# A vision-transformer tower on one core: by-query products and maxima 14 steps ahead of the by-key products in place of 16, and a head's maxima turned in its third step

## The reference

```python
h = _L0_tok_ref(x, ...)                       # gated token mixing, PReLU
h = h + _L0_attn_ref(_layernorm(h, axis=-1), ...)
h = h + _L0_ffn_ref(_layernorm(h, axis=-1), ...)   # 8 experts, top 2

# inside _L0_attn_ref, per image and head
attn = jnp.einsum('bnhd,bmhd->bhnm', q * scale, k)
attn = jax.nn.softmax(attn + bias[None], axis=-1)
out = jnp.einsum('bhnm,bmhd->bnhd', attn, v)
```

## Time and profile before

| | |
|---|---|
| Median of 3 runs | 548.75 us |
| The profiled execution's own time | 552.72 us |
| Its span | 550.9 us |
| Busy share over the span | PE 95%, DVE 83%, ACT 64%, POOL 16% |
| Share of the chain that ended last | PE 81%, DVE 8%, DMA 3%, issue 3% |
| Mean granted TensorE clock | 0.983 of full speed |

### The profile page before, as it was taken

One profiled execution on the slowest core, in us unless ns is written; L12 is line 12 of the kernel. 1 busy time (PEld: TensorE's weight loads), 2 busy tenths in 40 slices (PEclk: granted clock), 3 DMA queues, 4 the chain that ended last, 5 costly groups with the idle time before them and its releaser, 6 DMA issues.

```text
span 550.9 us, 12866 instructions
## 1 busy us (share of the span) xinstructions
PE 525.9 (95%) x4185; PEld 178.9 (32%) x4185; DVE 455.9 (83%) x539; ACT 355.0 (64%) x631; POOL 86.7 (16%) x184
## 2 busy tenths in 40 slices
PE   7999999889999999999999999999999989999996
PEld 5233333322333333333333333333333443233221
DVE  2678778987999999999999999999999676766644
ACT  2021222327898988988988989889888745445442
POOL 8701011324100001001001010010012340211000
PEclk9999999997999999999999999999999978999999
DMA  7600358691332323223223223233244000100001
GB/s 277 186 4 2 87 162 234 162 284 22 90 78 73 80 77 84 78 61 89 79 61 87 75 75 79 69 85 78 60 132 109 22 11 11 43 20 1 20 14 26
DMA packets 51095, 45.28 MB, mean 82 GB/s; under 512 B 26265, under 2 KB 39034, under 8 KB 51066
## 3 DMA queue, kind: packets, MB, share of 16 engines
q1 hardware_dynamic: 51066, 44.89, 29.0%
HBM read 28.70 MB, written 16.17 MB: 81 GB/s over the span
## 4 chain that ended last, share of the span: by engine, by line
PE 81%; DVE 8%; issue 3%; DMA 3%; SPq 2%; ACT 1%; POOL 1%; DVEq 0%; ACTq 0%; POOLq 0%
PE ps L1456 25%; PE ps L1352 13%; PE ps L1441 13%; PE ps L1533 5%; PE ps L1613 5%; PE ps L1275 4%; PE ps L1286 4%; DVE nmax L910 2%; DVE gated L931 1%; SPq L431 1%; PE ps L1445 1%; PE ps L1366 1%; PE ps L1600 1%; DMA maxima<-max_t 1%; DMA q_ring<-maxima 1%
## 5 line engine op out<-in xcount | busy, mean ns | idle before, releaser
L910 DVE TENSOR_REDUCE nmax<-ps 128x1 f32<-128x1024 f32 x256 | 302.2, 1218 | 19.8 <-PE ps L1352 11.3
L763 ACT ACTIVATE probs<-ps 128x512 f32<-128x512 f32 x512 | 278.1, 596 | 56.3 <-PE ps L1441 46.5
L1456 PE MATMUL ps<-probs,v_ring 128*32 128x256 f32 x2048 | 166.3, 398 | 0.0
L1441 PE MATMUL ps<-q_ring,k_ring 51*128 51x512 bf16 x512 | 101.8, 387 | 6.3 <-DMA q_ring<-maxima 2.0
L1352 PE MATMUL ps<-k_ring,q_ring 48*128 48x512 bf16 x512 | 100.5, 389 | 1.0 <-DVE nmax L910 0.7
L1456 PEld LDWEIGHTS ps<-probs,v_ring 128*32 128x32 f32 x2048 | 40.7, 108 | 63.8 <-issue 38.0
L1183 DVE TENSOR_TENSOR probs<-probs,ps 128x1024 f32<-128x1024 f32 x32 | 39.0, 1220 | 25.1 <-PE ps L1600 19.6
L1352 PEld LDWEIGHTS ps<-k_ring,q_ring 48*128 48x128 bf16 x512 | 24.6, 92 | 106.4 <-issue 99.4
L779 ACT ACTIVATE probs<-ps,wide_w 128x1024 f32<-128x1024 f32 x32 | 35.4, 1113 | 33.6 <-PE ps L1533 32.5
L931 DVE SCALAR_TENSOR_TENSOR gated<-ps,v_s,gamma_sb 128x1024 f32<-128x1024 f32 x32 | 40.8, 1281 | 12.3 <-PE ps L1275 10.9
L605 POOL TENSOR_TENSOR max_p<-nmax,zeros 128x8 bf16<-128x8 f32 x32 | 6.4, 200 | 274.7 <-DVE nmax L910 260.9
(11 more groups left out here) (168 smaller groups left out, 338.7 us busy)
## 6 DMA issues: line engine op xcount, KB each, us to landing
k_ring<-qk_parts SPq DMA_DIRECT2D x64, 96.0 KB, 2.4
q_ring<-qk_parts SPq DMA_DIRECT2D x64, 96.0 KB, 2.4
gamma_sb<-gamma_t SPq DMA_DIRECT2D x4, 1024.0 KB, 8.8
v_padded<-v_pad SPq DMA_DIRECT2D x4, 1024.0 KB, 5.8
v_ring<-v_padded SPq DMA_DIRECT2D x32, 128.0 KB, 3.2
outputs<-o_t SPq DMA_DIRECT2D x32, 128.0 KB
qk_parts<-qk_h SPq DMA_DIRECT2D x8, 384.0 KB, 4.6
x_ring<-bias_parts SPq DMA_DIRECT2D x32, 96.0 KB, 3.0
```

Of the source, the lines that this page charges most:

```text
L763: A.activation(probs[:, s % 4, HALF * j:HALF * (j + 1)], ps[:, key_bank(s, j), :], ACT.Exp).then_inc(exp_done[j], 1)
L910: V.tensor_reduce(nmax[:, par, s:s + 1], ps[:, bank:bank + 2, :].rearrange("p a n -> p (a n)"), AX, ALU.max, negate=True).then_inc(s1_redu ...
L1441: last = mm(ps[:, key_bank(s, j), :], k_ring[rows, u, P * s:P * (s + 1)], q_ring[rows, u, HALF * j:HALF * (j + 1)], start=True, stop=not c ...
L1456: last = mm(ps[VC * j:VC * (j + 1), PVB, 0:2 * P], v_ring[:, u, m, :], probs[:, m % 4, 2 * P * j:2 * P * (j + 1)], start=(m == 0), stop=(m ...
```

## The change

By-query products and their reductions run `LEAD = 14` steps ahead of the by-key products. Steps 0 and 1 of head g now carry by-query steps 6 and 7 of head g+1, and steps 2 to 7 carry steps 0 to 5 of head g+2. Two by-query steps fewer stand ahead of the loop, and head 30 carries the last two. The turn of head g+1's maxima moves from step 0 of head g to step 2. The place where the rows are waited for (step 7) stays, and so does SP's program. The first projection of the next stage is issued whole in step 2 of head 30, and no longer in two halves in steps 1 and 2. In after, a line number behind the added lines is 5 or 6 higher.

```diff
--- before.py
+++ after.py
@@ -295,6 +295,11 @@
         out_stored = [sem(f"out_stored{i}") for i in range(2)]
 
         N_OPERANDS = 5
+        LEAD = 2 * NT - 2
+
+        def by_query(s):
+            return 1 + (s + LEAD - NT) // NT, (s + LEAD) % NT
+
         N_MAX_ROWS = 16
         S1A, S2A, PVB = 0, 4, 7
 
@@ -1023,7 +1028,7 @@
             rest_part(B - 1)
             first_maxima(6, 9)
             turn_maxima(0, 0, None)
-            first_maxima(9, 2 * NT)
+            first_maxima(9, LEAD)
 
 
             def invert_sums(b):
@@ -1057,11 +1062,12 @@
                 for u in range(RING):
                     g = it * RING + u
                     for s in range(NT):
-                        if not (last and u >= RING - 2):
-                            if s == 0:
-                                dve.wait_ge(max_split, g + 1)
-                            row_max(g + 2, s, u % 2)
-                        if s == 0 and not (last and u == RING - 1):
+                        ahead, step = by_query(s)
+                        if not (last and u + ahead >= RING):
+                            if step == 0:
+                                dve.wait_ge(max_split, g + ahead - 1)
+                            row_max(g + ahead, step, (u + ahead) % 2)
+                        if s == 2 and not (last and u == RING - 1):
                             turn_maxima(g + 1, (u + 1) % 2, None if first and u == 0 else
                                         ((u + 1) % 2, it * (2 * N_MAX_ROWS) + (u + 1) // 2 * N_MAX_ROWS))
                         if last and (u, s) == (0, 3):
@@ -1428,9 +1434,9 @@
             first_scores(6, 7)
             keep_busy(5)
             project_vv(B - 1)
-            for i in range(7, 2 * NT):
+            for i in range(7, LEAD):
                 first_scores(i, i + 1)
-                keep_busy(3 if i < 2 * NT - 2 else 0)
+                keep_busy(3 if i < LEAD - 2 else 0)
             pe.wait_ge(qk_r_ready, B)
             pe.wait_ge(v_pad_ready, B)
 
@@ -1534,7 +1540,7 @@
                               start=True, stop=True)
                 last.then_inc(up_done, 1)
 
-            WITHIN = {(2, 1): (project_attention, 0, FIRST), (2, 2): (project_attention, 0, SECOND),
+            WITHIN = {(2, 2): (project_attention, 0, WHOLE),
                       (2, 3): (project_attention, 1, FIRST), (2, 4): (project_attention, 1, SECOND),
                       (2, 5): (project_attention, 2, FIRST), (2, 6): (project_attention, 2, SECOND),
                       (2, 7): (turn_norm, 0, WHOLE), (3, 0): (logits, 0), (3, 1): (turn_norm, 1, FIRST),
@@ -1544,11 +1550,10 @@
             def attend_pe(it, first, last):
                 for u in range(RING):
                     g = it * RING + u
-                    ahead = not (last and u >= RING - 2)
                     start, end = first and u == 0, last and u == RING - 1
                     v = (u + 1) % RING
                     pe.wait_ge(values_loaded[u], it * 16 + 16)
-                    if ahead:
+                    if not (last and u >= RING - 2):
                         pe.wait_ge(operands[(u + 2) % RING],
                                    (it + (u + 2) // RING) * (16 * N_OPERANDS) + 16 * N_OPERANDS)
                     if start:
@@ -1573,9 +1578,10 @@
                             values(it, g - 1, NT - 1, (u - 1) % RING)
                         if s > 1:
                             values(it, g, s - 2, u)
-                        if ahead:
-                            scores_upper(g + 2, s, (u + 2) % RING)
-                            scores_lower(g + 2, s, (u + 2) % RING)
+                        ahead, step = by_query(s)
+                        if not (last and u + ahead >= RING):
+                            scores_upper(g + ahead, step, (u + ahead) % RING)
+                            scores_lower(g + ahead, step, (u + ahead) % RING)
                         if last and (u, s) in WITHIN:
                             stage, *args = WITHIN[u, s]
                             stage(*args)
```

## The result

| | before | after |
|---|---|---|
| Median | 548.92 us (4 runs) | 624.32 us (4 runs, 622.33 to 628.97) |
| Ratio to before | | 1.139 (1.134 to 1.143) |
| Span of the profiled execution | 550.9 us | 620.5 us |
| Mean granted clock | 0.983 | 0.937 |
| PE, DVE, ACT busy | 95, 83, 64% | 89, 74, 57% |

The account below looks back on a forecast made before the run. PE was taken to bound the loop at 10.08 us a head; 27 × 1.43 = 38.6 plus 3.0 at the ends gave 41.6 over 548.75, or 590 us. Likeliest case 584 to 600, wider range 568 to 622.

Parts of the forecast that it names:

- The standstill: PE waits 1.6 us for the rows of maxima before step 7 in every head; period 11.51 us against 10.08.
- Granted clock 1.00 from head 1 to 29: Expected sign in the profile after: TensorE keeps full clock in heads 1 to 29 despite the idle time at step 7.
- the half clock: Rival: idle PE at step 7 drops TensorE's clock to 0.50, 25 to 47 us more, 615 to 637; chance 0.19.
- The price of a fall: TensorE at half clock for 6.7 us in every second head, costing 3.4 each, less up to 1.6 taken in.
- the rule on throttled time: Skill's reckoning for TensorE: a throttled stretch costs its length × (1 − K/N), half at K/N = 4/8.
- The second transfer at 2.80: The load of the maxima's rows takes 2.80 us from issue to landing, so they land at t + 10.30.
- The lighter-transfer rival: Rival: the load of the maxima's rows takes only 2.0 us; period 10.72, total 569 us; chance 0.14.
- The first transfer: After the turn, 2.02 us between the two issues, agreeing with the skill's nearly constant 2.0 us for a small DMA.
- The corner, 0.22 us a head less work: Three small products moved from step 0 to step 2 fill PE's wait for ACT, 0.22 us less a head.
- Ahead of the loop nothing gained: Two by-query steps leave, but the first by-key product still waits for head 0's rows at 123.98: no gain.
- The last heads: Heads 28, 29 and 30, at the loop's end, lengthen by 1.1, 0.7 and 0.7 us.
- DMA a fifth or more of the chain: Expected sign in the profile after: DMA makes up a fifth or more of the chain that ended last.

Follow-up runs that it names:

- the filler: Six products of 128x512 with unused results on TensorE ahead of step 7's wait for the rows, added to the changed kernel: 592.81 us, ratio 1.079.
- The turn alone: Kernel before, products still 16 steps ahead, with only the turn of the maxima moved from step 0 to step 2: 631.65 us, ratio 1.151.
- one filler: One product of 128x512 with unused result on TensorE ahead of step 7's wait for the rows, added to the changed kernel: 593.57 us, ratio 1.080.
- with 15 ahead: Changed kernel with products 15 steps ahead, turn in step 1, and SyncE loading the maxima's rows before the outputs' store and values' load: 542.82 us, ratio 0.986.
- with 14: Changed kernel, still 14 steps ahead, with SyncE loading the maxima's rows before the outputs' store and values' load: 551.19 us, ratio 1.002.

## Why the prediction was wrong

- **The standstill** (right). Its place, its releaser and nearly its size: 1.6 us forecast, 1.56 to 1.81 in the loop's heads without a fall. They take 11.6 to 11.8 us, where 11.51 was forecast; what is over is mostly PE's start behind the landing, 0.23 us and not 0.05. With the filler a head takes 11.52. Filler minus before, 592.8 − 549.6 = 43.2 us, is the term that was forecast as 41.6. The turn alone reproduces the standstill.
- **Granted clock 1.00 from head 1 to 29** (wrong). This is the step that failed: the half clock stood among the rivals with 0.19 and belonged in the sum. From head 5 on the clock fell in about three of four heads. After minus filler, 624.3 − 592.8, is **31.5 us**, nearly the whole miss of 33.8 (75.4 − 41.6); at least 25 of it are the clock's and about 3 go with PE's later start. The argument took comfort from a stretch of before with a gap of 1.12 us that held the clock, and from products of full length on both sides of the gap. The runs show that the change of a few tenths in the gap goes with the fall: 1.24 to 1.29 (heads 1 to 3) hold it and about 1.3 (one filler) nearly always, 1.56 to 1.93 lose it in about three of four heads. They don't show that the gap's length alone decides: with the turn alone 1.42 to 1.51 lost it too, and within one run the heads that fall don't have the longest gaps. The cause of the beat of three heads with and one without stays open.
- **The price of a fall** (right in kind, length wrong). The rival took 6.7 us at half clock from head 0; in the loop it is 3.4, 1.7 lost, and only 0.2 of that is taken in by the standstill, because the fall comes behind the gap, on the path to the next turn. 17 stretches × 1.7 = 29. By the rule on throttled time that was named with this rival (the Trainium skill, "TensorE: Matmul & The Clock Gate", section "Terms"), 58 us × (1 − 0.5) = 29; the 17 heads are 25 us longer in the trace, so it agrees but for what the standstill takes in. The rival had 25 to 47 us on top of 590, so its 615 to 637 held the time, partly by luck: falls were more frequent than its one in two and half as long.
- **The second transfer at 2.80** (right, 2.85 to 2.98), and why: alone it takes 1.4, so half of it is the traffic in front of it. The lighter-transfer rival needed SP's order changed to come true; the operand loads' distance did not do it.
- **The first transfer.** The 2.02 us were the distance of two issues, and the sum needs no more. But in the loop the chain runs there through SP's own issues (its queue is 8% of the chain), so this distance is only a bound on the transfer. Where the chain runs through the transfer, in heads 1 to 3, it takes 1.92 to 1.95 us. The section of the Trainium skill that the prediction names beside this ("DMA: Bandwidth & Descriptors", "Anatomy of one DMA — SWDGE (gpsimd) path") describes GpSimd's path, and these transfers are SyncE's; the figures are near each other, the paths are not the same.
- **The corner, 0.22 us a head less work** (right for the way to step 7: in heads 1 to 3 the gap is 1.24 to 1.29 us, and 1.05 to 1.09 with the turn alone). As a gain in time, once nothing waits for rows, it came out as 0.27 with 15 ahead but only 0.08 with 14. **Ahead of the loop nothing gained** (right): the first turn stayed at 116.8 us (117.0 before).
- **The last heads** (a little low). With the six fillers the last three distances of turns are 1.4, 1.0 and 1.4 us longer than before, 3.8 in all, where 1.1, 0.7 and 0.7 were forecast for heads 28 to 30.
- **DMA a fifth or more of the chain** (wrong): 16%, with 8% in SP's queue beside it.

## What to carry to other kernels

Before a producer is moved later in a software pipeline, follow its result through every hop to the wait it feeds and subtract: here 1.0 us of slack against a move of 2.4. A standstill on TensorE has two prices, the gap and the clock behind it; when the gap comes out longer than any that the trace shows at full clock, the second price belongs in the sum, and a cheap filler product in the gap shows its size, less what the filler changes besides (here PE's start behind the landing). Small transfers on a critical path go ahead of large ones in the queue; the same reorder is worth nothing where nothing waits.

## What the runs showed beyond that

- The answer was steep: one product of 128x512 (0.2 us) in a gap of 1.7 us gave 30.8 us over the kernel (624.32 to 593.57).
- The same two transfers with the same bytes take 4.9 to 5.0 us from the turn to the landing in heads 1 to 3, whose addresses are fixed, and 5.1 to 5.2 in the heads of the loop (4 to 27). SP's issues of the two are 1.94 to 1.97 us apart in the former and 2.02 to 2.28 in the latter.
- In heads 4 to 27 PE starts 0.23 us behind the landing when nothing was issued in the gap, and 0.05 when a filler product was. In heads 1 to 3 it is 0.05 without a filler, and 0.04 in head 28, behind the loop. Why is not shown.
